# One register load for all block counts, and a first expert block that runs row unit by row unit

## What is computed

```python
h = _layernorm(x, axis=-1) * (1 + cb) + sb                       # cb, sb: modulation vectors
gate_probs = jax.nn.softmax(h @ Wg + bg, axis=-1)                # 8 experts
_, top_idx = jax.lax.top_k(gate_probs, 2)
expert_mask = jax.nn.one_hot(top_idx, 8).sum(-2)
selected = gate_probs * expert_mask
selected = selected / (selected.sum(-1, keepdims=True) + 1e-08)
hid = jax.nn.gelu(jnp.einsum('bsf,efh->bseh', h, W1) + b1)       # 256 -> 1024
expert_out = jnp.einsum('bseh,ehf->bsef', hid, W2) + b2          # 1024 -> 256
x = x + gb * jnp.einsum('bsef,bse->bsf', expert_out, selected)
```

## Time and profile before

| what | value |
|---|---|
| median of 3 runs | 838.02 us (837.62 to 838.34) |
| the profiled execution, its own time | 837.4 us |
| its span, first to last instruction | 835.7 us |
| busy: PE | 760.6 us (91%) |
| busy: DVE, ACT, POOL | 611.4, 465.7, 341.3 us |
| chain that ended last: PE, DVE, issue | 74%, 16%, 5% |
| mean granted clock of TensorE | 0.955 |

### The profile page before, as it was taken

The page is one execution under the profiler, slowest core; times in us unless marked ns, Lnnn a source line. Parts: engine busy times, 40 slices in busy tenths (PEclk is TensorE's granted clock), DMA queues, the critical chain, the costliest instruction groups (busy, mean ns, idle before and its releaser), DMA issues.

```text
span 835.7 us, 16912 instructions
## 1 busy us (share of the span) xinstructions
PE 760.6 (91%) x5848; PEld 698.2 (84%) x5848; DVE 611.4 (73%) x1309; ACT 465.7 (56%) x841; POOL 341.3 (41%) x293
## 2 busy tenths in 40 slices
PE   5889999999999889956099999999999999999993
PEld 4777777888887679955099999999999999999992
DVE  6899999989899524799165867777676876876652
ACT  4464665665644413276076566665666666765461
POOL 2332332323322012100326566565656566666553
PEclk9999999999999999975599999999999999999997
DMA  7400000000000135423406263535326235233332
GB/s 285 151 1 1 1 2 2 2 1 1 2 1 1 52 115 193 163 60 79 134 17 157 52 153 61 144 63 143 64 46 159 46 66 138 52 46 57 59 52 39
DMA packets 45651, 59.72 MB, mean 71 GB/s; under 512 B 8018, under 2 KB 38804, under 8 KB 45460
## 3 DMA queue, kind: packets, MB, share of 16 engines
q0 software_dynamic: 14400, 21.98, 14.8%
q1 hardware_dynamic: 31188, 36.93, 13.6%
HBM read 40.63 MB, written 18.27 MB: 70 GB/s over the span
## 4 chain that ended last, share of the span: by engine, by line
PE 74%; DVE 16%; issue 5%; POOL 2%; DMA 1%; ACT 1%; SPq 0%; DVEq 0%; POOLq 0%; ACTq 0%
PE ps L1603 23%; PE ps L1617 22%; PE ps L1425 7%; PE ps L1383 6%; PE ps L1508 3%; PE ps L1446 3%; DVE at_hi L1189 2%; PE ps L1580 2%; PE ps L1434 2%; DVE q_max L912 2%; DVE q_sum L919 2%; DVE k_blk L1022 2%; PE ps L1528 1%; DVE q_exp L913 1%; DVE ln_s L876 1%
## 5 line engine op out<-in xcount | busy, mean ns | idle before, releaser
L825 ACT ACTIVATE hid<-ps,b_col 128x256 f32<-128x256 f32 (+1 forms) x232 | 106.1, 509 | 110.3 <-PE ps L1603 64.7
L1617 PE MATMUL ps<-w_hi,hid_hi 128*128 128x256 f32 x544 | 153.6, 282 | 0.0
L1617 PE MATMUL ps<-w_lo,hid_hi 128*128 128x256 f32 x544 | 151.3, 278 | 0.0
L1617 PE MATMUL ps<-w_hi,hid_lo 128*128 128x256 f32 x544 | 151.3, 278 | 0.0
L1603 PE MATMUL ps<-xT_hi,w_hi 128*128 128x256 f32 (+1 forms) x464 | 140.5, 303 | 9.9 <-issue 9.9
L1303 DVE TENSOR_TENSOR hid_lo<-hid,hid_hi 128x512 fp32r<-128x512 f32 (+1 forms) x116 | 91.0, 784 | 73.8 <-ACT hid_hi L829 71.1
L1603 PE MATMUL ps<-xT_lo,w_hi 128*128 128x256 f32 (+1 forms) x464 | 140.1, 302 | 0.0
L1603 PE MATMUL ps<-xT_hi,w_lo 128*128 128x256 f32 (+1 forms) x464 | 140.1, 302 | 0.0
L588 POOL DMA_INDIRECT out<-y,y_id x68 | 117.0, 1721 | 38.7 <-POOL y_id L583 22.2
L527 POOL TENSOR_TENSOR q_n<-q_exp,q_rec 128x1024 f32<-128x1024 f32 x32 | 61.0, 1905 | 174.7 <-DVE q_rec L920 174.7
L576 POOL DMA_INDIRECT listed<-xrows,gid x93 | 101.8, 1095 | 45.2 <-POOL gid L572 26.3
(11 more groups left out here) (206 smaller groups left out, 1478.8 us busy)
## 6 DMA issues: line engine op xcount, KB each, us to landing
w_raw<-in_L_ffn_W SPq DMA_DIRECT2D x16, 1024.0 KB
x_all<-in_L_attn_x SPq DMA_DIRECT2D x8, 512.0 KB, 9.4
out<-x_all SPq DMA_DIRECT2D x8, 512.0 KB, 3.0
xrows<-x_all SPq DMA_DIRECT2D x8, 512.0 KB, 4.7
listed<-xrows,gid POOLq DMA_INDIRECT x93
out<-y,y_id POOLq DMA_INDIRECT x68
wqk_raw<-in_L_attn_w_qkv SPq DMA_DIRECT2D x2, 512.0 KB, 6.2
wqk_raw<-in_L_attn_w_qkv SPq DMA_DIRECT2D x1, 1024.0 KB, 10.5
```

Source lines behind the costliest of these rows:

```text
L825: ins = act.activation(hid[:, m, 0:T], src, ACT.Gelu_apprx_tanh, bias=b1_col[:, e, m:m + 1])
L1617: last = pe.matmul(ps[:, bank, 0:D], a, w_, start=m == 0 and st, stop=m == M - 1 and sp_)
```

## The change

It has these parts.

- `wide` and `narrow` become two halves of one tile `plan`, and `block_numbers` reads all sixteen values with one register load per engine, directly after `s_counts`; the checks move to a `snap` at each expert's start.
- `count_blocks` moves behind the conversion of the index to `ids`, which is done in two pieces, first 6 columns (two blocks of three units), then the other 250. `s_idxr` rises after each piece.
- The first gather uses `ids` directly, without `gid`, with one semaphore per unit (`s_row0`); so does the second, still on `s_rows`. DVE normalizes, PE transposes (into three pairs of PSUM banks, `XT0`), ACT modulates and DVE splits one unit at a time.
- The `pad` stores move to POOL's free time after the weight split of expert 0; the weights of expert 1 move up to SP's place after the sixth chunk; the load of `b2_bc` waits for the three first gathers, and DVE's wait for it moves to just ahead of the expert loop.
- ACT runs one gelu on a column of constants (`warm`) before the seam.

In the instruction streams: PE ahead of the first expert loop. Before, the transposes come first and then sixteen loads, of which the first two stand here with their checks.

Both `gid` copies of this place are gone, and the `pad` stores stand ahead of the wait for the counts. The diff, without the semaphore declarations and the loop's renumbered waits:

```diff
@@
+        plan = sb("plan", [P, 2 * E], I32)
+        wide, narrow = plan[:, 0:E], plan[:, E:2 * E]
+        warm = sb("warm", [P, 1], F32)
...
+        XT0 = (4, 6, 0)
...
-        def block_numbers(eng):
-
-            return [(eng.value_load(wide[0:1, e:e + 1], min_val=1, max_val=2),
-                     eng.value_load(narrow[0:1, e:e + 1], min_val=1, max_val=N // P // 2)) for e in range(E)]
...
+        def block_numbers(eng, name):
+
+            regs = [eng.alloc_register(f"plan{i}_{name}") for i in range(2 * E)]
+            eng.reg_load(regs, plan[0:1, :])
+            return regs
...
             for e in range(E):
-                three, two = numbers[e]
+                three = eng.snap(regs[e], min_val=1, max_val=2)
+                two = eng.snap(regs[E + e], min_val=1, max_val=N // P // 2)
                 body(e, e % 2, three, two, e == E - 1)
...
                 store_x1(c)
                 store_rows(c)
+                if c == GCH + 1:
+                    sp.wait_ge(s_wlo, 1)
+                    load_weights(1)
                 if c == GCH + 2:
                     store_weights(0)
             store_weights(1)
-            sp.wait_ge(s_wlo, 1)
-            load_weights(1)
-            sp.wait_ge(s_idxr, 1)
+            sp.wait_ge(s_idxr, 2)
+            for i in range(BI):
+                sp.wait_ge(s_row0[i], 16)
...
+            pool.wait_ge(s_pad, 1)
+            for i in range(BI):
+                pool.dma_start(out[N + i * P:N + (i + 1) * P, :], pad[:, i, 0:D]).then_inc(s_added, 16)
+
             for c in range(CHUNKS):
                 pool.wait_ge(s_xo[c], 16)
+            pool.wait_ge(s_xr, 16 * (BI + CHUNKS + GROUPS))
+            pool.wait_ge(s_idxr, 1)
+            for i in range(BI):
+                pool.indirect_dma_start(listed[:, i, :], None, xrows[:, :],
+                                        bass.IndirectOffsetOnAxis(ap=ids[:, i:i + 1], axis=0)).then_inc(s_row0[i], 16)
             pool.wait_ge(s_counts, 1)
-
+            numbers = block_numbers(pool, "pool")
+            pool.wait_ge(s_meta, 1 + ONE)
+            pool.wait_ge(s_bt, BI)
             for i in range(BI):
-                pool.dma_start(out[N + i * P:N + (i + 1) * P, :], pad[:, i, 0:D]).then_inc(s_added, 16)
+                pool.indirect_dma_start(listed[:, i, :], None, xrows[:, :],
+                                        bass.IndirectOffsetOnAxis(ap=ids[:, BI + i:BI + i + 1], axis=0)).then_inc(s_rows, 16)
+            pool.wait_ge(s_idxr, 2)
...
+            act.wait_ge(s_const, CONSTS)
+            act.activation(warm[:, :], mean_w[:, 0:1], ACT.Gelu_apprx_tanh)
             act.wait_ge(s_counts, 1)
+            numbers = block_numbers(act, "act")
...
-            block_full(0)
-
-            numbers = block_numbers(act)
+            for i in range(BI):
+                act.wait_ge(s_bt, i + 1)
+                for c in range(C):
+                    act.activation(xT_full[:, c, i * P:(i + 1) * P], ps[:, XT0[i] + c, 0:P], ACT.Identity,
+                                   bias=modc[:, 2, c:c + 1], scale=modc[:, 3, c:c + 1]).then_inc(s_bfull, 1)
...
+            dve.wait_ge(s_idx, CHUNKS)
+            for cols in (slice(0, 2 * BI), slice(2 * BI, E * COLS)):
+                link(dve.scalar_tensor_tensor(pad_t[:, cols], ps[:, IX, cols], 0.0, pad_row[:, cols], ALU.is_ge, ALU.mult))
+                dve.scalar_tensor_tensor(ids[:, cols], ps[:, IX, cols], float(N), pad_t[:, cols], ALU.add, ALU.add).then_inc(s_idxr, 1)
             count_blocks()
...
+            dve.wait_ge(s_counts, 1)
+            numbers = block_numbers(dve, "dve")
...
-            take(0)
-            take_third()
-            block_parts(0)
+            for i in range(BI):
+                dve.wait_ge(s_row0[i], 16)
+                normalize(i).then_inc(s_norm, 1)
+            dve.tensor_copy(y_next[:, :, :], listed[:, :, D:D + E]).then_inc(s_meta, 1)
+            for i in range(BI):
+                r = slice(i * P, (i + 1) * P)
+                for c in range(C):
+                    dve.wait_ge(s_bfull, i * C + (c + 1))
+                    link(dve.tensor_copy(xT_hi[:, c, r], xT_full[:, c, r]))
+                    last = dve.tensor_tensor(xT_lo[:, c, r], xT_full[:, c, r], xT_hi[:, c, r].bitcast(F32), ALU.subtract)
+            last.then_inc(s_blo, 1)
             chain.end()
-            numbers = block_numbers(dve)
+            dve.wait_ge(s_b2, 16)
...
             pe.wait_ge(s_counts, 1)
+            numbers = block_numbers(pe, "pe")
...
-            block_T(0)
-
-            numbers = block_numbers(pe)
+            for i in range(BI):
+                pe.wait_ge(s_norm, i + 1)
+                for c in range(C):
+                    last = pe.transpose(ps[:, XT0[i] + c, 0:P], listed[:, i, c * P:(c + 1) * P], ident[:, :])
+                last.then_inc(s_bt, 1)
+
```

More of the change, by code:

```diff
@@ L120, in adaln_block @@
         parity = sb("parity", [P, E], I32)
-        wide = sb("wide", [P, E], I32)
-        narrow = sb("narrow", [P, E], I32)
+        plan = sb("plan", [P, 2 * E], I32)
+        wide, narrow = plan[:, 0:E], plan[:, E:2 * E]
+        warm = sb("warm", [P, 1], F32)
         tick = sb("tick", [P, 1], F32)
@@ L320, in adaln_block @@
         s_rows = sem("s_rows")
+        s_row0 = [sem(f"s_row0_{i}") for i in range(BI)]
         s_meta = sem("s_meta")
@@ L390, in after, with experts @@
                 eng.wait_ge(sem_, count)
-        def block_numbers(eng):
-            return [(eng.value_load(wide[0:1, e:e + 1], min_val=1, max_val=2),
-                     eng.value_load(narrow[0:1, e:e + 1], min_val=1, max_val=N // P // 2)) for e in range(E)]
-        def experts(numbers, body):
+        def block_numbers(eng, name):
+            regs = [eng.alloc_register(f"plan{i}_{name}") for i in range(2 * E)]
+            eng.reg_load(regs, plan[0:1, :])
+            return regs
+        def experts(eng, regs, body):
             for e in range(E):
-                three, two = numbers[e]
+                three = eng.snap(regs[e], min_val=1, max_val=2)
+                two = eng.snap(regs[E + e], min_val=1, max_val=N // P // 2)
                 body(e, e % 2, three, two, e == E - 1)
@@ L569, in gather @@
                 pool.wait_ge(s_meta, n + ONE)
-                pool.wait_ge(s_bt, n + ONE)
+                pool.wait_ge(s_bt, n + BI - 1)
                 pool.sem_inc(s_turn_pool, 1)
                 pool.tensor_copy(gid[:, :], ids[:, bass.ds(col, BI)]).then_inc(s_gid, 1)
-                pool.wait_ge(s_gid, n + 1)
+                pool.wait_ge(s_gid, n - 1)
                 pool.sem_inc(s_turn_pool, 1)
@@ L590, in scatter @@
                 pool.reg_add(u, u, size)
[L592 to L596, removed]
             at = pool.alloc_register("at_pool")
@@ L627, in expert @@
                     pool.reg_add(g, g, 1)
-            experts(numbers, expert)
+            experts(pool, numbers, expert)
             pool.wait_ge(s_added, now(pool, u) * 16 + DMA3)
-            pool.wait_ge(s_rows, now(pool, g) * 48 + 2 * DMA3)
+            pool.wait_ge(s_rows, now(pool, g) * 48 + DMA3)
             pool.sem_inc(s_done, 1)
@@ L791, in _ @@
                 lo_hot(c)
+            act.wait_ge(s_const, CONSTS)
+            act.activation(warm[:, :], mean_w[:, 0:1], ACT.Gelu_apprx_tanh)
             act.wait_ge(s_counts, 1)
+            numbers = block_numbers(act, "act")
             g = block_counter(act, "g_act")
             def block_full(n):
-                act.wait_ge(s_bt, n + 1 + ONE)
+                act.wait_ge(s_bt, n + BI)
                 for c in range(C):
@@ L841, in expert @@
                     rows_block(2, False)
-            experts(numbers, expert)
+            experts(act, numbers, expert)
         @block.vector
@@ L1226, in _ @@
                 hi_hot(c)
-            count_blocks()
             dve.tensor_scalar(ids[:, E * COLS:E * COLS + BI - 1], pad_row[:, E * COLS:E * COLS + BI - 1], float(N), None, ALU.add)
             dve.wait_ge(s_idx, CHUNKS)
-            link(dve.scalar_tensor_tensor(pad_t[:, :], ps[:, IX, 0:E * COLS], 0.0, pad_row[:, 0:E * COLS], ALU.is_ge, ALU.mult))
-            dve.scalar_tensor_tensor(ids[:, 0:E * COLS], ps[:, IX, 0:E * COLS], float(N), pad_t[:, :], ALU.add, ALU.add).then_inc(s_idxr, 1)
-            dve.wait_ge(s_b2, 16)
+            for cols in (slice(0, 2 * BI), slice(2 * BI, E * COLS)):
+                link(dve.scalar_tensor_tensor(pad_t[:, cols], ps[:, IX, cols], 0.0, pad_row[:, cols], ALU.is_ge, ALU.mult))
+                dve.scalar_tensor_tensor(ids[:, cols], ps[:, IX, cols], float(N), pad_t[:, cols], ALU.add, ALU.add).then_inc(s_idxr, 1)
+            count_blocks()
+            dve.wait_ge(s_counts, 1)
+            numbers = block_numbers(dve, "dve")
             g = block_counter(dve, "g_dve")
@@ L1243, in block_parts @@
                 for c in range(C):
-                    dve.wait_ge(s_bfull, n * C + (c + 1))
+                    dve.wait_ge(s_bfull, n * C + ((BI - 1) * C + c + 1))
```

(12 more changed lines are left out.)

## The result

The changed kernel takes 831.83 us (median of 4 runs, 831.42 to 833.31) against 838.13 for the kernel before beside it, a ratio of 0.993 (95% interval 0.9917 to 0.9943). It is faster, by 6.3 us, but the forecast was 10.4 us, to 827.6, and the range ended at 831.0. The profiled execution took 831.79 us, of which 830.0 is span; before, 837.4 and 835.7.

What follows compares the result with a forecast made beforehand. PE was taken as the bound, so an earlier first expert matmul should arrive whole: 11.1 us, less 0.3 for gathers and 0.4 for the clock, gives 10.4, to 827.6 us; range 825.8 to 831.0.

Steps and rivals of the forecast that it cites:

- Ids and gather: Seam's start: 6-column index conversion without the `gid` copy starts the first gather at 398.15; third unit lands at 403.62.
- 0.3 us set aside for contention: First three gathers: deduction for DVE being busy beside their issues, at most 1.1 us for three.
- Counts and load: After the index: counts end at 400.40, then one register load of length L, free on the path up to 2.5 us.
- rival of a load that costs by the value: Register load: sixteen values at single-load price, L 10.24, 835.3 us; at half price 5.1, 830.2 us; chance 0.13.
- Row units: After the third landing: six cast-and-subtract pairs at 0.50 take 3.0 us (2.5 to 5.5); PE starts at 407.3.
- What moved: Moved expert 1 weights, `meta` store, `b2_bc` load, second gathers and early gelu: all at no cost; `b2_bc` lands at 409.1.
- bias rival: Expert loop's start: DVE waits for a late `b2_bc`, landing at 415.1 and costing 2.5 us, 830.1 us; chance 0.05.
- Clock: First expert matmuls: PE's low-clock stretch may lose 1.15 us more than before or gain up to 1.65.
- 0.4 set aside: First expert matmuls: deduction in us for PE's clock possibly staying low longer than before.
- first paragraph: What bounds the kernel: PE, busy all 382.30 us from 437.70 to 820.00, so an earlier expert start arrives whole.
- from there to the end the same length as before: Sign for the new trace: the stretch from PE's first expert matmul, near 407.3, to the end is unchanged.
- a wait that I don't see: Unplaced remainder: an unseen wait that may fall on either side of the forecast; chance 0.02.

Runs made afterwards that it cites:

- after_noshift: The changed kernel with `warm` and `tick` as two columns of one tile, so every other tile keeps its old address: 825.46 us, ratio 0.9853.
- shift_only: The kernel before with one unused 4-byte tile where the changed kernel has `warm`, no instruction different: 843.79 us against 837.81, ratio 1.0073.
- hid_shift: after_noshift with the hidden tiles 32 bytes lower and the weights where they were: 832.07 us, ratio 0.9934.
- after_hid224: The changed kernel with the hidden tiles 224 bytes lower, by unused bytes ahead of them: 828.47 us, ratio 0.9885.
- place_e: after_noshift with 192 unused bytes ahead of the first layer's inputs, weights and hidden tiles unmoved: 822.9 us, ratio 0.9813.

## Why the prediction was right in the seam and wrong in the sum

**Ids and gather.** Right. First gather 398.21 (forecast 398.15), third unit normalized at 403.65 (403.62). The 0.3 us set aside for contention weren't lost: the issues took 1.03, 0.98 and 0.95 beside DVE's small instructions, against a median of 0.98. The rule of the Trainium skill, "SBUF — State Buffer", section "SBUF: two separate sides", that GpSimd can't write DMA descriptors while VectorE holds the port that they share, shows no cost that can be read here. There the rule is tied to certain instructions of VectorE; whether those beside these gathers are among them, no run shows.

**Counts and load.** Right. L is 1.35 us, inside the 2.5 that the path had room for, so DVE still waited 0.75 for the third unit. The rival of a load that costs by the value (10.24, or half of it) falls. The figure of the Trainium skill, "Runtime: NRT & Kernel Launch", section "Instruction fetch mechanics", about 200 ns a register, doesn't carry over to this load: 1.35 / 16 = 84 ns. The Trainium skill tells it, by the section "Terms" of the same page, of register loads from HBM, and `plan` lies in SBUF, so the prediction's 3.2 us rested on a figure for another kind of load.

**Row units.** Right, a little on the careful side: cast and subtraction come in pairs 0.46 us apart (404.07 to 404.53), forecast 0.50. PE started at 406.98, forecast 407.3.

**What moved.** Right. `b2_bc` (`b_bc` in the views) landed just ahead of 409.10 (forecast 409.1) and held up DVE's loop by 2.17 us, but no wait of PE followed. The bias rival didn't happen.

**Clock.** Right in kind; the 0.4 set aside wasn't lost. The granted clock was again 0.50 over the first matmuls, and their 48 took 10.10 us, against 10.17 before (9.96 to 11.11 in the other runs); the stretch behind is at 0.98 (us, PE, PEld, DVE, ACT, POOL, clock, DMA, GB/s):

```profile
407.00:410.10 3.10, 3.10 (x10) 3.10 (x11) 0.85 (x2) 0.55 (x1) 1.74 (x2) 0.50 0.56 180
410.10:415.00 4.90, 4.90 (x29) 4.90 (x28) 2.73 (x4) 3.80 (x6) 0.00 (x0) 0.98 0.05 18
```

**The step that failed** is the first paragraph's: "every microsecond by which the first expert matmul comes earlier should arrive at the end whole, as long as PE doesn't wait later". PE didn't wait later, and the gain didn't arrive whole. The sentence takes PE's pace as given, and the sum has no term for it: the 382.30 us of PE work were read as a constant. So its own sign, "from there to the end the same length as before", failed by 5.7 us. Over all experts PE's work became 6.1 us longer, because a tile named only for its instruction ("ACT's early gelu lies in its wait") also took 32 bytes of memory. The edit was costed by what it issues and not by what it allocates. Without that term the forecast would have been on the other side: 837.4 - 11.4 - 0.1 = 825.9 for the profiled execution, and after_noshift, where the term is gone, has a median of 825.46, just below the range. The forecast of 827.6 was slow by its two allowances, 0.7 together, and by 0.3 at the row units; the rest, 1.1, is no more than after_noshift's four runs differ (823.49 to 826.64). The chance of 0.02 for "a wait that I don't see" was the only place for it, and it wasn't a wait.

**What stays open.** That the extra slot of 32 bytes costs the 6 us is shown: put into the old kernel it costs them (shift_only), and without it the changed kernel doesn't lose them (after_noshift). That it acts by the relative place of the two operands is supported, by moving the hidden tiles in place of the weights (hid_shift), by moving them until the distance is 256 bytes more, which gives back two thirds (after_hid224), and by the first layer, which holds its pace when both operands move together. It isn't the whole rule: after_hid224 is 2.1 us short of the old pace, and in place_e the second layer became 2 us slower with none of its operands moved. Why 32 bytes do it, what the period is, whether the two reads of PE meet each other or the reads and writes of other engines on the same tiles, and what chooses between 3.41 and 3.54 us for the same 30 matmuls, these runs don't tell.

## What to carry to other kernels

Where PE is the bound and has no gaps, look at the pace of its matmuls before and after an edit, not at its waits alone: count and sum of one line's pieces in the chain show a loss of 3% that no wait shows. An allocation is part of a change: keep the addresses of the operands of the hot loop fixed (put a new small tile into an existing slot, or behind them), or an edit far from the loop is judged by a shift that it causes. And sixteen loads of single values are best made into one.

## What the hardware showed that was not expected

- The 1602 matmuls of the second layer took 116.0 ns each at the old place (185.9 us in all), 119.8 with the moving operand 32 bytes further from the stationary one (192.0), and 118.6 with 64 (190.0). A narrow block of the first layer took 5.44 to 5.76 us at the places that were tried.
- One unused tile of 4 bytes made the old kernel 6.0 us slower; 192 unused bytes at another place made the changed one with `warm` out of the way about 2.6 us faster (822.9 against 825.46), the fastest of the kernels that were timed in several runs.
- One register load of sixteen values took 1.35 us, where a single one had cost 0.62 to 0.64 with its checks.
